# Expert products of a two-layer language-model tower on one core: the 64-row up products of a group issued together ahead of the 128-row ones, with six PSUM banks for up and one for down

## Chip, core and metric

The kernel runs on one core of a Trainium2 chip. The metric is device time in microseconds (us) of one execution. The kernel before takes 2085.38 us (median of 3 runs, 2085.08 to 2086.68).

## What is computed

The reference embeds 32 x 128 tokens in 192 dimensions and sends them through two layers, each an attention and a feed-forward part. Everything touched here lies in the last part, the mixture of experts of the second layer:

```python
T = B * S                                   # 4096 tokens, D = 192
logits = xm @ router_w.T + router_b         # E = 8 experts
topw, topi = jax.lax.top_k(softmax(logits), 2)
topw = topw / jnp.sum(topw, axis=-1, keepdims=True)
for e in range(E):
    h = gelu(xm @ w1[e] + b1[e], approximate=False)   # 192 -> 768
    y = h @ w2[e] + b2[e]                             # 768 -> 192
    out = out + combine[:, e:e + 1] * y
x = x + out
```

## The kernel before

**The expert part.** While layer 2 is computed, every token's normed row is written twice to a table in HBM (`xs`), ordered by expert. The expert part goes through this table in 39 groups (`NX`) of 256 rows (`NR`), each of one expert. Three groups make one turn of a hardware loop (`TURNS` is 13, `B3` is 3), and weights, rows, turned rows and outputs have three buffers each, number `h` for a group's place in its turn. All products are fp32; in the profile one fp32 `matmul` is two MATMUL records and two LDWEIGHTS records, and a transpose is one of each.

**A group's work.** The input dimension 192 is 128 + 64 and the hidden dimension 768 is six blocks of 128 (`FC`), taken in three pairs (`PAIRS`), blocks `p` and `p + 3`.

- SyncE (`sync_x`, L2245) loads the group's weights (L2258, six transfers) and its rows (L2262) three groups ahead: it waits for `x_out`, the end of the outputs of the group that had this buffer.
- VectorE `doubled` (L2217) copies the rows' last 64 columns when the rows have landed, so that both halves of the partitions get them.
- TensorE `turn_rows` (L2291, L2292) turns the next group's rows with four transposes into bank 6; ScalarE `take_rows` (L2350) takes them out as `x_T`, two instructions.
- TensorE `up` (L2296), once for each pair: two products of 128 rows (L2307, one for each block) and two of 64 rows (L2311). The two of 64 rows use partitions 0 to 63 and 64 to 127, so they lie in different halves of the array, and they end the sums that the two of 128 rows begin.
- ScalarE (L2359) applies gelu to the pair, two instructions, and counts `x_gelu`.
- TensorE `down` (L2315), once for each pair: four products of 128 rows and 192 columns (L2322), two row tiles `t` for each block, summed over the six blocks in banks 4 and 5.
- VectorE `outputs` (L2198) adds the weighted bias and the weighted result (L2204 to L2211), counts `x_out`, and GpSimd (`pool_x`, L2236) adds the rows into `moe_sum` in HBM with two indirect DMAs (L2240). It waits until both have landed before it takes the next group. An output buffer is used again three groups later, and `outputs` waits for that (L2200).

**What sets the order.** TensorE works in program order, written out in `group_of` (L2327): up 0, up 1, turn of the next group, down 0, up 2, down 1, down 2. Banks 0 and 1 serve pairs 0 and 2, banks 2 and 3 pair 1, so up 2 waits for the gelu of pair 0 (L2303). `down` waits for the gelu of its pair (L2316), and down 0 also for `x_out` of the group before (L2318), which frees banks 4 and 5. ScalarE takes the next group's rows between the gelus of pairs 1 and 2 (L2362).

```python
            def group_of(g, h, more, first=False):
                up(g, h, 0, first)
                up(g, h, 1)
                if more:
                    turn_rows(*((g, h + 1) if h < B3 - 1 else (g + 1, 0)))
                down(g, h, 0)
                up(g, h, 2)
                down(g, h, 1)
                down(g, h, 2)
```

Of the kernel before, what the change touches and what calls it, by code (L numbers as in the profile page):

```python
# [11 lines left out]
ACT = mybir.ActivationFunctionType  # L12
# [4 lines left out]
P = 128  # L17
T = 32
D = 192
# [6 lines left out]
TE, HE = 3, 64  # L26
# [9 lines left out]
def per(g, n, k):  # L36

    return g * n + k
# [57 lines left out]
def tower(nc, a, out):  # L96

    with ExitStack() as ctx:
# [2036 lines left out]
        B3 = 3  # L2135
# [33 lines left out]
        def vector_x(v, ch):  # L2169

            nc.vector.memset(amx[:, :], 0.0).then_inc(x_sel_r, 1)
            v.wait_ge(x_pos_p, 1)
            tot = bank[0][:, 400:400 + E]
            ch.step(nc.vector.tensor_scalar(x_steps, l_cnt[:, 0:NP], NR + 1 / 32, -NR - 3 / 64, ALU.mult, ALU.add))
            ch.step(nc.vector.tensor_tensor(x_more, tot.unsqueeze(2).to_broadcast([P, E, NP]),
                                            x_steps.unsqueeze(1).to_broadcast([P, E, NP]), ALU.is_gt))
            ch.step(nc.vector.tensor_reduce(x_ng, x_more, X, ALU.add))
            ch.step(nc.vector.tensor_copy(x_end, x_ng))
            for e in range(1, E):
                ch.step(nc.vector.tensor_tensor(x_end[:, e:e + 1], x_end[:, e:e + 1], x_end[:, e - 1:e], ALU.add))  # L2180
            group = l_cnt[:, 0:NX]
            ch.step(nc.vector.tensor_tensor(x_which, group.unsqueeze(2).to_broadcast([P, NX, E]),
                                            x_end.unsqueeze(1).to_broadcast([P, NX, E]), ALU.is_gt))
            ch.step(nc.vector.tensor_reduce(x_ex, x_which, X, ALU.add))
            nc.vector.tensor_scalar(x_from, x_ex, float(E - 1), None, ALU.min)
            ch.step(nc.vector.tensor_tensor(x_whose, x_which, x_ng.unsqueeze(1).to_broadcast([P, NX, E]), ALU.mult))
            nc.vector.tensor_copy(x_exi, x_from)
            ch.step(nc.vector.tensor_reduce(x_row, x_whose, X, ALU.add))
            ch.step(nc.vector.tensor_tensor(x_row, group, x_row, ALU.subtract))
            ch.step(nc.vector.tensor_scalar(x_row, x_row, -1.0, float(NR), ALU.add, ALU.mult))  # L2190
            ch.step(nc.vector.scalar_tensor_tensor(out=x_row, in0=x_ex, scalar=float(T * P), in1=x_row, op0=ALU.mult, op1=ALU.add))
            ch.step(nc.vector.tensor_scalar(x_row, x_row, float(E * T * P), None, ALU.min))
            nc.vector.tensor_copy(x_rowi, x_row).then_inc(x_read, 1)
            ch.step(nc.vector.memset(amx[:, :], 0.0))
            nc.vector.memset(amx[:, :], 0.0).then_inc(x_out, 1)
            ch.clear()

            def outputs(g, h, first=False):  # L2198
                if not first:
                    v.wait_ge(x_add, per(g, 32 * B3, 32 * (h - 2)))  # L2200
                w = lambda t: x_in[h][:, t, 1:2]
                v.wait_ge(x_w[h], per(g, 96, 96))
                for t in range(NT):
                    nc.vector.tensor_scalar(x_y[h][:, t, :], xb_2[h], w(t), None, ALU.mult)  # L2204
                ch.step(nc.vector.scalar_tensor_tensor(out=x_z[h], in0=x_in[h][:, :, 1], scalar=0.0, in1=r_dump, op0=ALU.is_equal,
                                                       op1=ALU.mult))
                ch.step(nc.vector.tensor_tensor(x_z[h], x_z[h], x_in[h][:, :, 0], ALU.max))
                nc.vector.tensor_copy(x_id[h], x_z[h])
                v.wait_ge(x_dn, per(g, B3, h + 1))
                for t in range(NT):  # L2210
                    ins = nc.vector.scalar_tensor_tensor(out=x_y[h][:, t, :], in0=bank[4 + t][:, 0:D], scalar=w(t),  # L2211
                                                         in1=x_y[h][:, t, :], op0=ALU.mult, op1=ALU.add)
                ins.then_inc(x_out, 1)

            def doubled(g, h):
                v.wait_ge(x_x[h], per(g, 16, 16))
                nc.vector.tensor_copy(x_in[h][:, :, WID:WID + HE], x_in[h][:, :, WID - HE:WID]).then_inc(x_dup, 1)  # L2217

            doubled(0, 0)
            for h in range(B3):  # L2220
                doubled(*((0, h + 1) if h < B3 - 1 else (1, 0)))
                outputs(0, h, True)
            ch.step(nc.vector.memset(amx[:, :], 0.0))
            ch.clear()
            with v.Fori(1, TURNS - 1) as g:
                for h in range(B3):
                    doubled(*((g, h + 1) if h < B3 - 1 else (g + 1, 0)))
                    outputs(g, h)
                ch.step(nc.vector.memset(amx[:, :], 0.0))
                ch.clear()  # L2230
            for h in range(B3):
                if h < B3 - 1:
                    doubled(TURNS - 1, h + 1)
                outputs(TURNS - 1, h)
# [10 lines left out]
        def sync_x(sp):  # L2245
# [35 lines left out]
            sp.dma_start(flat(out.rearrange("t p d -> (t p) d")), flat(acc[0:T * P, :])).then_inc(x_end_st, 16)  # L2281
            sp.wait_ge(x_end_st, 16)

        def tensor_x(pe):
            pe.wait_ge(x_sel_r, 1)
            nc.tensor.matmul(bank[0][:, 400:400 + E], r_ones, r_run, start=True, stop=True).then_inc(x_pos_p, 1)
# [6 lines left out]
                                             x_in[h][:, t, 2 + P:2 + 2 * P], ident[:, :])  # L2293
                mm.then_inc(x_turned, 1)

            def up(g, h, p, first=False):  # L2296
                if p == 0:
                    pe.wait_ge(x_xT, per(g, B3, h + 1))
                    pe.wait_ge(x_w[h], per(g, 96, 96))
                    if h > 0 or not first:  # L2300
                        pe.wait_ge(x_gelu, per(g, B3 * PAIRS, h * PAIRS))
                elif p == 2:
                    pe.wait_ge(x_gelu, per(g, B3 * PAIRS, h * PAIRS + 1))  # L2303
                b = (0, 2, 0)[p]
                for n in range(2):
                    q = p + PAIRS * n
                    nc.tensor.matmul(bank[b + n][:, 0:NR], xw_1a[h][:, q * P:(q + 1) * P], x_T[h][:, 0, :], start=True,  # L2307
                                     stop=False)
                for n in range(2):
                    s = slice(HE * n, HE * (n + 1))  # L2310
                    mm = nc.tensor.matmul(bank[b + n][:, 0:NR], xw_1b[h][s, p * P:(p + 1) * P], x_T[h][s, 1, :], start=False,  # L2311
                                          stop=True)
                mm.then_inc(x_up, 1)

            def down(g, h, p):  # L2315
                pe.wait_ge(x_gelu, per(g, B3 * PAIRS, h * PAIRS + p + 1))  # L2316
                if p == 0:
                    pe.wait_ge(x_out, per(g, B3, h + 1))  # L2318
                for n in range(2):
                    f = p + PAIRS * n  # L2320
                    for t in range(NT):
                        mm = nc.tensor.matmul(bank[4 + t][:, 0:D], x_hid[f][:, t * P:(t + 1) * P], xw_2[h][:, f, :],  # L2322
                                              start=(p == 0 and n == 0), stop=(p == PAIRS - 1 and n == 1))
                if p == PAIRS - 1:
                    mm.then_inc(x_dn, 1)

            def group_of(g, h, more, first=False):  # L2327
                up(g, h, 0, first)
                up(g, h, 1)
                if more:  # L2330
                    turn_rows(*((g, h + 1) if h < B3 - 1 else (g + 1, 0)))
                down(g, h, 0)
                up(g, h, 2)
                down(g, h, 1)
                down(g, h, 2)

            turn_rows(0, 0)
            for h in range(B3):
# [7 lines left out]
        def scalar_x(act):  # L2346
            def take_rows(g, h):
                act.wait_ge(x_turned, per(g, B3, h + 1))
                for c in range(2):
                    ins = nc.scalar.activation(x_T[h][:, c, :], bank[6][:, c * NR:(c + 1) * NR], ACT.Identity,  # L2350
                                               scale=x_ln2g[:, c:c + 1], bias=x_ln2b[:, c:c + 1])
                ins.then_inc(x_xT, 1)

            def group_of(g, h, more):
                for p in range(PAIRS):
                    act.wait_ge(x_up, per(g, B3 * PAIRS, h * PAIRS + p + 1))
                    for n in range(2):
                        q = p + PAIRS * n
                        ins = nc.scalar.activation(x_hid[q], bank[(0, 2, 0)[p] + n][:, 0:NR], ACT.Gelu,  # L2359
                                                   bias=xb_1[h][:, q:q + 1])  # L2360
                    ins.then_inc(x_gelu, 1)
                    if p == 1 and more:  # L2362
                        take_rows(*((g, h + 1) if h < B3 - 1 else (g + 1, 0)))

            take_rows(0, 0)
            with act.Fori(0, TURNS - 1) as g:
# [139 lines left out]
```

## Time and profile before

| what | value |
|---|---|
| median of 3 runs | 2085.38 us (2085.08 to 2086.68) |
| profiled execution: span from first to last instruction | 2106.3 us |
| profiled execution: own time | not given apart from its span |
| TensorE busy with matmuls, of the span | 1611.5 us (77%) |
| first and last start of an expert product of 64 rows (L2311) | 1722.3 us and 2084.3 us |
| 64-row, 128-row up and down MATMUL records | 468, 468 and 936 |

The profile shows one execution. It gives for each engine its instructions with start and duration, and for the idle time before one what ended it. A MATMUL record's end is modelled; successive matmuls overlap, so the pace of a stream is read from starts, or from the chain of waits, which gives each instruction only the time that it adds. PE stands for matmuls of TensorE, PEld for its weight loads, DVE for VectorE, ACT for ScalarE, POOL for GpSimd, SP for SyncE. All times are counted from the span's start. The profiled execution's span is 20.9 us longer than the median run.

### The profile page before, as it was taken

The numbers are of one execution on the slowest core, as the hardware profiler recorded it, in microseconds if no ns is written. First come the engines' busy times: TensorE is split into PE (matmuls) and PEld (weight loads), VectorE is DVE, ScalarE is ACT, GpSimd is POOL, SyncE is SP. The second block draws the span as 40 slices with busy tenths as digits, with TensorE's granted clock in tenths as the row PEclk, the third lists the DMA queues.
The fourth block names the chain that finished last, engine by engine and source line by source line (L and its number), as shares of the span: only waits on it lengthen the run. The fifth ranks groups of instructions, "written<-read, shape, count | busy, mean of one in ns | idle before, by whom it ended". The sixth has DMA issues, their size and how long they took to land.

```text
span 2106.3 us, 35471 instructions
## 1 busy us (share of the span) xinstructions
PE 1611.5 (77%) x12060; PEld 1159.8 (55%) x12060; DVE 1312.3 (62%) x4361; ACT 979.3 (46%) x2773; POOL 400.4 (19%) x494
## 2 busy tenths in 40 slices
PE   0166764968888578888888768888888759999996
PEld 0032223855665355555555456666676647777775
DVE  7898885878888677877788536555555532122221
ACT  1366998933444445554555323333333324443442
POOL 7302331000000100000000001222212223333332
PEclk9975555578888689999999878777777769999998
DMA  3000001079910000000000000000000037777775
GB/s 71 15 1 1 1 1 20 3 141 193 188 20 0 1 1 0 0 0 0 0 0 0 1 25 13 24 23 23 23 15 19 23 96 179 185 175 181 177 176 133
DMA packets 136262, 112.99 MB, mean 54 GB/s; under 512 B 29417, under 2 KB 128457, under 8 KB 136137
## 3 DMA queue, kind: packets, MB, share of 16 engines
q1 hardware_dynamic: 119320, 91.70, 18.4%
q0 software_dynamic: 16864, 20.33, 5.0%
q8 instruction: 40, 0.66, 0.1%
q14 instruction: 38, 0.30, 0.1%
HBM read 69.19 MB, written 45.94 MB: 55 GB/s over the span
## 4 chain that ended last, share of the span: by engine, by line
PE 52%; DVE 27%; ACT 14%; issue 4%; POOL 1%; DVEq 0%; DMA 0%; another core or an unknown queue 0%; SPq 0%; ACTq 0%; POOLq 0%
ACT bank L716 8%; PE bank L2322 8%; PE bank L1007 6%; PE bank L2307 5%; PE bank L2311 3%; PE bank L1987 3%; PE bank L966 3%; PE bank L1217 2%; PE bank L1665 2%; PE bank L1000 2%; PE bank L2000 2%; DVE WK L1839 1%; DVE WK L1581 1%; DVE R L1581 1%; DVE R L1839 1%
## 5 line engine op out<-in xcount | busy, mean ns | idle before, releaser
L1047 POOL TENSOR_TENSOR WK<-WK,mhalf 128x2 f32<-128x2 f32 (+1 forms) x96 | 77.9, 812 | 882.4 <-DVE WK L1505 328.4
L2359 ACT ACTIVATE R<-bank,R 128x256 f32<-128x256 f32 x234 | 98.2, 471 | 216.9 <-PE bank L2311 216.9
L2211 DVE SCALAR_TENSOR_TENSOR WK<-bank,R,WK 128x192 f32<-128x192 f32 x78 | 28.9, 413 | 262.8 <-PE bank L2322 262.8
L716 ACT ACTIVATE bank<-bank,nbias,sc 128x128 f32<-128x128 f32 x384 | 168.9, 991 | 22.6 <-POOL nbias L528 22.6
L1007 PE MATMUL bank<-WK,R 96*128 96x256 f32 x576 | 162.9, 429 | 17.0 <-ACT WK L973 11.0
L2240 POOL DMA_INDIRECT moe_sum<-WK x78 | 121.5, 1557 | 257.4 <-DVE WK L2211 196.4
L2322 PE MATMUL bank<-R 128*128 128x192 f32 x936 | 169.1, 331 | 0.0
L716 ACT ACTIVATION_READ_ACCUMULATOR bank<-bank,nbias,sc 128x1 f32 x384 | 163.0, 766 | 0.0
L2322 PEld LDWEIGHTS bank<-R 128*128 128x128 f32 x936 | 150.1, 190 | 13.3 <-issue 13.3
L1007 PEld LDWEIGHTS bank<-WK,R 96*128 96x128 f32 x576 | 116.2, 213 | 41.9 <-ACT WK L973 15.4
L2307 PE MATMUL bank<-R 128*128 128x256 f32 x468 | 125.2, 390 | 1.1 <-ACT R L2350 1.1
L1987 PE MATMUL bank<-WK 32*128 32x128 f32 x1536 | 84.4, 367 | 35.4 <-DVE R L1839 13.0
L610 PE MATMUL bank<-R 32*128 32x128 bf16 x384 | 62.7, 299 | 60.0 <-ACT bank L716 57.1
L966 PE MATMUL bank<-ident,WK 128*96 128x128 f32 x320 | 66.4, 345 | 44.3 <-DVE WK L1030 27.7
L1987 PEld LDWEIGHTS bank<-WK 32*128 32x128 f32 x1536 | 69.2, 255 | 50.5 <-DVE R L1839 15.3
L2307 PEld LDWEIGHTS bank<-R 128*128 128x128 f32 x468 | 84.0, 191 | 20.9 <-issue 13.3
L610 PEld LDWEIGHTS bank<-R 32*128 32x128 bf16 x384 | 29.4, 118 | 118.7 <-ACT bank L716 106.6
L1665 PE MATMUL bank<-WK,R 128*128 128x256 f32 x256 | 75.6, 420 | 15.0 <-ACT WK L993 15.0
L433 DVE TENSOR_REDUCE neg_all<-bank 128x3 f32<-128x384 f32 x128 | 69.4, 554 | 27.4 <-PE bank L610 25.2
L559 PE MATMUL bank<-R,wq 96*128 96x512 bf16 x192 | 79.3, 542 | 4.6 <-DVE WK L407 2.7
L2311 PE MATMUL bank<-R 64*128 64x256 f32 x468 | 82.7, 430 | 0.0
L1000 PE MATMUL bank<-R,WK 96*128 96x192 f32 x384 | 76.4, 343 | 2.9 <-ACT WK L973 1.4
(494 smaller groups left out, 3886.4 us busy)
## 6 DMA issues: line engine op xcount, KB each, us to landing
moe_rows_in<-zeros SPq DMA_DIRECT2D x1, 25026.0 KB, 138.7
R<-in_L_ffn_w SPq DMA_DIRECT2D x39, 576.0 KB
R<-in_L_ffn_w SPq DMA_DIRECT2D x39, 384.0 KB
R<-moe_rows_in SPq DMA_DIRECT2D x39, 194.0 KB, 4.6
R<-in_L_ffn_w SPq DMA_DIRECT2D x78, 96.0 KB
R<-in_L_ffn_b SPq DMA_DIRECT2D x39, 96.0 KB
moe_sum<-resid POOLq DMA_DIRECT2D x16, 192.0 KB
moe_sum<-WK POOLq DMA_INDIRECT x78, 5.9
```

The lines of the kernel that those rows point to most:

```text
L610: mm = nc.tensor.matmul(bank[u % 4][:, k * P:(k + 1) * P], qk[32 * j:32 * j + 32, k, i * P:(i + 1) * P], qk[32 * j:32 * j + 32, 3 + k, i * ...
L716: ins = nc.scalar.activation(s, s, ACT.Exp, bias=nbias[:, u, k:k + 1], scale=col(SS), accum_out=units(sum_all, g, u)[:, k:k + 1])
L966: mm = nc.tensor.transpose(a.bank[b][0:C, c * NM + i * P:c * NM + (i + 1) * P], src[:, i, c * C:(c + 1) * C], ident[:, :])
L1000: mm = nc.tensor.matmul(a.bank[b][:, i * D:(i + 1) * D], a.xT[0:C, c, i * P:(i + 1) * P], w[0:C, c, :], start=(c == 0), stop=(c == 1))
L1007: mm = nc.tensor.matmul(out, w[0:C, c, m], a.xT[0:C, c, :], start=(c == 0), stop=(c == 1))
L1665: nc.tensor.matmul(a.bank[c][:, out], wa[:, c * P:(c + 1) * P], a.xT[:, 0, :], start=True, stop=False)
L1987: mm = nc.tensor.matmul(a.bank[j][:, k * P:(k + 1) * P], x, y, start=True, stop=True)
L2240: pool.indirect_dma_start(out=acc, out_offset=bass.IndirectOffsetOnAxis(ap=x_id[k % B3][:, t:t + 1].bitcast(U32), axis=0), in_=x_y[k % B3] ...
L2307: nc.tensor.matmul(bank[b + n][:, 0:NR], xw_1a[h][:, q * P:(q + 1) * P], x_T[h][:, 0, :], start=True, stop=False)
L2311: mm = nc.tensor.matmul(bank[b + n][:, 0:NR], xw_1b[h][s, p * P:(p + 1) * P], x_T[h][s, 1, :], start=False, stop=True)
L2322: mm = nc.tensor.matmul(bank[4 + t][:, 0:D], x_hid[f][:, t * P:(t + 1) * P], xw_2[h][:, f, :], start=(p == 0 and n == 0), stop=(p == PAIRS ...
L2359: ins = nc.scalar.activation(x_hid[q], bank[(0, 2, 0)[p] + n][:, 0:NR], ACT.Gelu, bias=xb_1[h][:, q:q + 1])
```

## The change

TensorE's order within a group becomes: all six 64-row products first (they now begin the sums), in three pairs, then the six 128-row ones, pair by pair (they end the sums and count `x_up`), then the turn of the next group's rows, then down 0, 1 and 2. The three pairs of up products have banks 0 to 5. The down products of both row tiles go to bank 7, columns 0 to 191 and 192 to 383; only the first of them has `start`. ScalarE does the gelus of all three pairs and then takes the next group's rows. The wait of up 2 for a gelu is gone; the 64-row products wait for the turned rows, the weights and all gelus of the group before, as up 0 did.

```diff
-                    ins = nc.vector.scalar_tensor_tensor(out=x_y[h][:, t, :], in0=bank[4 + t][:, 0:D], scalar=w(t),
+                    ins = nc.vector.scalar_tensor_tensor(out=x_y[h][:, t, :], in0=bank[7][:, t * D:(t + 1) * D], scalar=w(t),
...
+        def hidden_at(p, n):
+
+            return bank[2 * p + n][:, 0:NR]
...
-            def up(g, h, p, first=False):
-                if p == 0:
-                    pe.wait_ge(x_xT, per(g, B3, h + 1))
-                    pe.wait_ge(x_w[h], per(g, 96, 96))
-                    if h > 0 or not first:
-                        pe.wait_ge(x_gelu, per(g, B3 * PAIRS, h * PAIRS))
-                elif p == 2:
-                    pe.wait_ge(x_gelu, per(g, B3 * PAIRS, h * PAIRS + 1))
-                b = (0, 2, 0)[p]
+            def up_rests(g, h, first=False):
+                pe.wait_ge(x_xT, per(g, B3, h + 1))
+                pe.wait_ge(x_w[h], per(g, 96, 96))
+                if h > 0 or not first:
+                    pe.wait_ge(x_gelu, per(g, B3 * PAIRS, h * PAIRS))
+                for p in range(PAIRS):
+                    for n in range(2):
+                        s = slice(HE * n, HE * (n + 1))
+                        nc.tensor.matmul(hidden_at(p, n), xw_1b[h][s, p * P:(p + 1) * P], x_T[h][s, 1, :], start=True, stop=False)
+
+            def up(h, p):
                 for n in range(2):
                     q = p + PAIRS * n
-                    nc.tensor.matmul(bank[b + n][:, 0:NR], xw_1a[h][:, q * P:(q + 1) * P], x_T[h][:, 0, :], start=True,
-                                     stop=False)
-                for n in range(2):
-                    s = slice(HE * n, HE * (n + 1))
-                    mm = nc.tensor.matmul(bank[b + n][:, 0:NR], xw_1b[h][s, p * P:(p + 1) * P], x_T[h][s, 1, :], start=False,
-                                          stop=True)
+                    mm = nc.tensor.matmul(hidden_at(p, n), xw_1a[h][:, q * P:(q + 1) * P], x_T[h][:, 0, :], start=False, stop=True)
                 mm.then_inc(x_up, 1)
...
-                        mm = nc.tensor.matmul(bank[4 + t][:, 0:D], x_hid[f][:, t * P:(t + 1) * P], xw_2[h][:, f, :],
-                                              start=(p == 0 and n == 0), stop=(p == PAIRS - 1 and n == 1))
+                        mm = nc.tensor.matmul(bank[7][:, t * D:(t + 1) * D], x_hid[f][:, t * P:(t + 1) * P], xw_2[h][:, f, :],
+                                              start=(p == 0 and n == 0 and t == 0), stop=(p == PAIRS - 1 and n == 1),
+                                              skip_group_check=True)
...
             def group_of(g, h, more, first=False):
-                up(g, h, 0, first)
-                up(g, h, 1)
+                up_rests(g, h, first)
+                for p in range(PAIRS):
+                    up(h, p)
                 if more:
                     turn_rows(*((g, h + 1) if h < B3 - 1 else (g + 1, 0)))
-                down(g, h, 0)
-                up(g, h, 2)
-                down(g, h, 1)
-                down(g, h, 2)
+                for p in range(PAIRS):
+                    down(g, h, p)
...
-                        ins = nc.scalar.activation(x_hid[q], bank[(0, 2, 0)[p] + n][:, 0:NR], ACT.Gelu,
-                                                   bias=xb_1[h][:, q:q + 1])
+                        ins = nc.scalar.activation(x_hid[q], hidden_at(p, n), ACT.Gelu, bias=xb_1[h][:, q:q + 1])
                     ins.then_inc(x_gelu, 1)
-                    if p == 1 and more:
-                        take_rows(*((g, h + 1) if h < B3 - 1 else (g + 1, 0)))
+                if more:
+                    take_rows(*((g, h + 1) if h < B3 - 1 else (g + 1, 0)))
```

## Rows read from the trace of the kernel before

**Rows 1.** The page: span, busy time, slices, the chain by engine.

```profile
span 2106.3 us, 35471 instructions
...
PE   0166764968888578888888768888888759999996
...
PEclk9975555578888689999999878777777769999998
...
PE 52%; DVE 27%; ACT 14%; issue 4%; POOL 1%; DVEq 0%; DMA 0%; another core or an unknown queue 0%; SPq 0%; ACTq 0%; POOLq 0%
```

**Rows 2.** Busy time by stretch: PE, PEld, DVE, ACT, POOL, clock, DMA share, GB/s.

```profile
1880.00:1920.00 40.00, 40.00 (x224) 31.04 (x223) 8.66 (x36) 16.27 (x34) 12.42 (x8) 1.00 0.73 180
...
1881.30:1890.67 9.37, 9.37 (x54) 7.23 (x54) 1.91 (x8) 4.71 (x9) 3.10 (x2) 1.00 0.72 175
...
2040.00:2086.00 46.00, 46.00 (x255) 35.28 (x255) 9.28 (x40) 16.22 (x38) 15.61 (x10) 1.00 0.57 126
```

**Rows 3.** Chain of waits through one group: start, time it adds, instructions.

```profile
1881.62 0.86 PE bank L2307 x4
1882.48 0.63 PE bank L2311 x4
1883.11 1.06 PE bank L2307 x4
...
1884.81 0.26 PE bank L2291
1885.07 0.11 PE bank L2292
...
1885.39 1.30 PE bank L2322 x8
1886.70 0.86 PE bank L2307 x4
...
1888.19 2.80 PE bank L2322 x16
```

**Rows 4.** Durations of 64-row matmuls; a run of 32-row ones; their line's groups.

```profile
L2311 PE MATMUL bank<-R x468: 376/480/792, 1722.3 to 2084.3; 64*128 64x256 f32 x156
...
1559.49 1.67 PE L1987 MATMUL bank<-WK 32*128 32x128 f32 x24
...
L1987 PE MATMUL bank<-WK 32*128 32x128 f32 x480 | 26.9, 372 | 10.6 <-DVE R L1839 5.7 <-DVE WK L1839 3.1 <-DVE R L1870 1.1
...
L1987 PEld LDWEIGHTS bank<-WK 32*128 32x128 f32 x480 | 22.0, 260 | 15.2 <-DVE R L1839 6.5 <-DVE WK L1839 3.7 <-issue 3.0
```

**Rows 5.** Timeline of ScalarE in the same group.

```profile
1884.85 0.84 ACT L2359 ACTIVATE R<-bank,R 128x256 f32<-128x256 f32 x2 [0.85 <-PE bank L2311]
1885.58 1.02 ACT L2350 ACTIVATE R<-bank,R 128x256 f32<-128x256 f32 x2
...
1889.10 1.28 ACT L2359 ACT_TABLE_LOAD   x1
```

**Rows 6.** VectorE in the same group, and its waits for rows from 1750 to 2080.

```profile
1881.65 0.74 DVE L2211 SCALAR_TENSOR_TENSOR WK<-bank,R,WK 128x192 f32<-128x192 f32 x2 [6.63 <-PE bank L2322]
1882.95 0.23 DVE L2217 COPY R<-R 128x128 f32<-128x128 f32 x1 [0.55 <-DMA R<-moe_rows_in]
...
DVE R L2217 <- DMA R<-moe_rows_in: 21.2, 32, 1.2
```

**Rows 7.** GpSimd's adds: timeline, landing times (min/median/max), waits, and issues at the end.

```profile
1883.16 1.55 POOL L2240 DMA_INDIRECT moe_sum<-WK  x1 [5.96 <-DVE WK L2211]
1885.01 1.55 POOL L2240 DMA_INDIRECT moe_sum<-WK  x1 [0.30 <-issue]
...
DMA to landing us min/median/max: 3.3/5.9/7.2
...
POOL moe_sum L2240 <- DMA moe_sum<-WK: 35.7, 6, 6.0
...
moe_sum<-WK POOLq DMA_INDIRECT x6, 3.5
```

## The prediction

> **What bounds the kernel now.** The page comes first [rows 1]: the six slices that lie wholly in the expert part, the 34th to the 39th of 40, show TensorE busy for nine tenths or more and its granted clock at nine tenths or more, while the half-clock stretches lie earlier. The table by stretch says it sharply [rows 2]: in every stretch of the expert part TensorE's matmuls fill the whole time (40.00 of 40.00, 46.00 of 46.00 us) at clock 1.00, the 2.4 GHz level, while VectorE, ScalarE and GpSimd are at a fifth, two fifths and a third, and the DMA engines at 0.73. So this part lasts as long as TensorE's own list of matmuls takes, and only what shortens that list counts. The chain of waits then prices the list piece by piece [rows 3]; the group from 1881.62 takes 9.37 us.
>
> Its pieces, in order: up 0 is 0.86 for the 128-row records and 0.63 for the 64-row ones; up 1 is 1.06 and 0.63; the turn 0.26 and three times 0.11; down 0 1.30; up 2 0.86 and 0.63; downs 1 and 2 2.80. Sum 9.36. Equal work is not priced equally: four 128-row records are 0.86 (0.215 each) where they follow other 128-row work (up 0 and up 2, both after a down), but 1.06 after 64-row work. Sixteen down records after 64-row work are 2.80, though eight are 1.30 after a transpose, so 2.60 was due. The first transpose is 0.26 against 0.11. And a 64-row block is 0.63 where its halves, running side by side, stream two records' time, 0.43. **Each passage between 64-row and 128-row work thus costs about 0.20 us** (0.15 before a transpose); the group has six. It isn't a wait for a bank: the transposes write bank 6 and the downs bank 4, which the 64-row products before them do not touch, and both pay; up 2 after down 0 changes banks and pays nothing. Part of it is seen in the records: the first matmuls of a 64-row block last 480 ns and the later ones 376 [rows 4], so about 0.10 is a weight load that nothing hides, and the rest the emptying of the array.
>
> **The change part by part.**
>
> *The order on TensorE.* The same records are issued, in two runs instead of six. New group: 64-row pairs 0.63 + 0.43 + 0.43 = 1.49; 128-row pairs 1.06 + 0.86 + 0.86 = 2.78; turn 4 x 0.11 = 0.44; downs 3 x 1.30 = 3.90. Sum 8.61 against 9.36, so **0.75 us a group**. With 39 groups (468 MATMUL records of 64 rows, twelve a group [rows 4]) that is 29.3 us. Worked out the other way, by taking 0.20 for each of the four passages that go, it is 31.2; I take the first, as it prices the transposes' passage at its own row. The price that no row shows directly is the 64-row pair that follows another pair: 0.43 if its loads hide behind the pair before. Bounds: 0.43 (nothing but streams) and 0.53 (each new pair shows the 0.10 of load). The nearest row is a run of 32-row products, 24 records in 1.67 us [rows 4]: four quarters of the array side by side, in six rounds. Less one record's length of 0.37 that is 0.22 a round, under the 0.26 of a single load there, so loads into a busy quarter are hidden. I take 0.43.
>
> *What down 0 waits for.* The gelus of pair p cover 0.84 us [rows 5], and up delivers pairs 0.86 apart, so ScalarE keeps pace. Counted as the chain counts, from the group's start: up 0 is out at 2.6, its gelu done at 3.5, and down 0 has its place from 4.7 (its first load some 0.3 earlier); gelu 1 is done at 4.3, needed at 5.7; gelu 2 at 5.2, needed at 7.0. At least 0.9 us cover each. The two output instructions of the group before end 0.8 us after the group's start [rows 6], also long before down 0. The removed wait of up 2 had cost nothing.
>
> *take_rows after the third gelu.* It starts at 5.2 and takes 1.02 [rows 5], done at 6.2, and the next 64-row products want it at 8.3: cover 2.1. The table load of 1.28 us [rows 5], once a turn, then ends at 7.5, and the next gelu starts at 11.2. Cost nothing; without the cover it would be what take_rows is late.
>
> *The turn, and the rows it needs.* It moves from 3.2 to 4.3 us after the group's start. Rows are asked for by the outputs three groups back, and a group is 0.75 shorter, so the copy on VectorE comes later within its group: now it waits at most 1.2 us after the outputs [rows 6] and ends 2.2 us after the group's start at the latest, then near 3.0. The slack before the turn stays at about 1 us at worst. Behind the turn only the downs are queued. VectorE has time: 1.9 us of work in 9.37 [rows 2].
>
> *SyncE and the DMA engines.* The same loads in less time: 0.72 of 9.37 is 6.7 us of work, or 0.78 of 8.61. No new instruction, nothing is moved past another there.
>
> *Bank 7 for both row tiles.* VectorE reads the same number of elements. TensorE already sends records in direct succession into one bank (the two passes of each product), so I cost it at nothing, with 0 to 0.02 a record as bounds: a full 0.02 x 24 x 39 = 19 us would be seen at once.
>
> *GpSimd, the one cover that gets thin.* A group's adds are two issues 1.86 us apart, the second landing 5.9 (median) to 7.2 us (longest) after it [rows 7]: 7.8 to 9.1 from the first issue, and some 0.3 to the next (what lies between the two issues). In the window of the waits row the landing ended GpSimd's wait only 6 times; else the outputs did, at a pace of 9.37. At 8.61 it will be the landing more often. The range is 8.1 to 9.4, and I take 8.7, since the second issue, behind the first, should land later than the median of both. GpSimd may fall behind without hurting anyone (output buffers return three groups later), and after the last loads the landings take 3.5 [rows 7], so that some 2.5 us a group is caught up in three groups, 7.5 in all. The lag at 8.7 is 35 x 0.09 = 3: nothing is left at the end.
>
> *Sum.* 29.3 us. The profiled span is 2106.3 and the execution's own time is not given apart from it, so the sum is made as a difference: 2106.3 becomes 2077.0. The span stands 1.0% above the median run; the same difference from 2085.4 gives **2056 us** (29.0 if it shrinks with that ratio).
>
> **A rule against this.** In the 64-row pair the second set of loads does not delay its matmuls: the block costs 0.43 plus one passage [rows 3], and six rounds of 32-row work run through [rows 4]. The Trainium skill, in "TensorE: Matmul & The Clock Gate", Part 3, says that a weight load overlaps running matmuls only when it targets another row group. By that rule the pairs put next to each other would each show their loads; the rows speak against it, and it is kept as rival B.
>
> **Rivals.**
>
> *A, GpSimd sets the pace.* Denser DMA traffic lengthens the landings, and the adds take 9.0 to 9.4 us a group. For it: six waits already end on a landing. Against it: traffic of a group is one burst, and a lagging GpSimd lands in its gap. The last add then comes 35 x (9.2 - 8.61) - 7.5 = 13 us late: 2069 (2062 at 9.0, 2076 at 9.4). Chance 0.13.
>
> *B, loads of 64-row pairs show.* Two more unhidden loads of 0.10 a group, 8 us: 2064. Chance 0.05.
>
> *C, the change does not do what it says.* If the 0.20 hung on something else than the passage (the sums of one bank, say), it would return in the new order: 2085. The transposes and downs that pay without sharing a bank speak against it. Chance 0.02.
>
> *D, slower.* The same GpSimd wait, past its point of decision: all adds a group over 8.61 + (29.3 + 7.5) / 35 = 9.66 us. With landings at 7.2 x 0.78 / 0.72 = 7.8 each time, a group takes 1.86 + 7.8 + 0.3 = 9.96, which gives 35 x 1.35 - 7.5 = 40 us on 2056: 2096. It needs the longest landing in every group. Chance 0.03.
>
> **How the numbers follow.** The main case has 0.77, and its own spread is 2053 (31.2 saved and a little at the first group, where up 2 now runs ahead of rows that are late) to 2060 (a part of bank 7's bound). The range takes in B and the middle of A: 2052 to 2069. Within 0.2% (4 us, about what a measurement can tell from no change) lies C: 0.02. Slower is D: 0.03. Faster 0.95.
>
> **What would show it.** In the chain of waits after: one 64-row piece of twelve records at about 1.5 us a group, then twelve 128-row up records at about 2.8, a first transpose at 0.11, and 3.9 for 24 down records; 8.6 us a group with TensorE still filling each stretch. ScalarE's take_rows after three gelus with more than 2 us before the next group. GpSimd's waits ended by landings more often, by outputs less. B would show as 1.7 in the 64-row piece; A as a chain that ends in DMA and GpSimd over many groups, and more than 7 us between TensorE's last matmul and the copy of the result. TensorE idle before the turn for late rows, or a group above 8.8 us, would make the prediction wrong.

## The result, and the profile after

The changed kernel takes 2055.7 us (median of 4 runs, 2055.25 to 2057.09), the kernel before 2086.0 (4 runs, 2085.08 to 2086.8): a ratio of 0.9855, interval 0.9841 to 0.9869. That is 30 us less, where 29.3 were forecast.

Busy time by stretch, after (columns: stretch, PE, PEld, DVE, ACT, POOL, clock, DMA share, GB/s):

```profile
1830.00:1838.62 8.62, 8.62 (x53) 7.61 (x53) 2.11 (x8) 3.44 (x8) 2.73 (x2) 1.00 0.81 194
...
1780.00:1820.00 40.00, 40.00 (x245) 35.59 (x246) 8.56 (x35) 17.44 (x39) 13.73 (x9) 1.00 0.81 199
```

Against [rows 2] nothing has changed its place: TensorE still fills every microsecond at clock 1.00. Only the list is shorter, 8.62 us a group instead of 9.37. The DMA engines were busy for 0.68 to 0.75 of each stretch of 40 us inside the expert part, and are so now for 0.78 to 0.81 (0.78 forecast). The chain of waits, after, through one group:

```profile
1824.18 3.90 PE bank L2323 x24
1828.08 1.50 PE bank L2308 x12
1829.58 2.79 PE bank L2313 x12
1832.36 0.11 PE bank L2295
1832.47 0.11 PE bank L2296
1832.58 0.11 PE bank L2295
1832.69 0.11 PE bank L2296
```

The reader sees each term of the sum: 1.50 for the twelve 64-row records (1.49 forecast), 2.79 for the 128-row up records (2.78), four times 0.11 for the turn, whose first transpose cost 0.26 in [rows 3], and 3.90 for the downs. The three 0.63 pieces of [rows 3] have become one piece that pays the 0.20 of a passage once.

How far the covers hold, from the timeline of the same group (start, length, instructions, idle time before and what ended it):

```profile
1828.12 0.74 DVE L2211 SCALAR_TENSOR_TENSOR WK<-bank,R,WK 128x192 f32<-128x192 f32 x2 [5.05 <-PE bank L2323]
...
1829.62 1.55 POOL L2240 DMA_INDIRECT moe_sum<-WK  x1 [5.21 <-DMA moe_sum<-WK]
1829.98 0.23 DVE L2217 COPY R<-R 128x128 f32<-128x128 f32 x1 [1.10 <-DMA R<-moe_rows_in]
...
1830.67 2.57 ACT L2360 ACTIVATE R<-bank,R 128x256 f32<-128x256 f32 x6 [3.84 <-PE bank L2313]
...
1832.20 0.27 PE L2295 MATMUL bank<-ident,R 128*128 128x128 f32 x1
...
1832.64 4.07 PE L2323 MATMUL bank<-R 128*128 128x192 f32 x24
1833.13 1.02 ACT L2351 ACTIVATE R<-bank,R 128x256 f32<-128x256 f32 x2
1836.63 1.57 PE L2308 MATMUL bank<-R 64*128 64x256 f32 x12
```

The six gelu instructions run as one piece of 2.57 us and end at 1833.24; the next group's rows are taken by 1834.15, and TensorE wants them at 1836.63: 2.5 us of cover, 2.1 forecast. The copy of the rows ends at 1830.21, 2.0 us before the turn; from the third group on this slack is 1.0 to 3.2 us, 1.9 in the median. The waits, after, from 1730 to 2025 (who waited for what: us in total, times, longest):

```profile
POOL moe_sum L2240 <- DMA moe_sum<-WK: 161.3, 31, 6.0
DVE R L2217 <- DMA R<-moe_rows_in: 41.1, 34, 2.1
POOL moe_sum L2240 <- DVE WK L2211: 15.6, 3, 5.2
```

Against the 6 waits of [rows 7], 31 of GpSimd's are now ended by a landing, as forecast, and yet no time was lost to it. Most of them cost GpSimd nothing either: in 25 of the 39 groups the adds begin at most 0.8 us after the outputs end, which is also the usual time in the kernel before, where the outputs decide; in the other 14 they begin up to 0.9 us later than that. VectorE waits for rows up to 2.1 us, 0.9 longer than in [rows 6].

**Two profiles that differ elsewhere.** The two spans differ by 52.6 us (2106.3 and 2053.7), far more than the 30 us of the runs. The first copy of the expert part stands at 1717.8 us before and at 1694.7 after, though no instruction ahead of it was changed (rows of the copies and of the outputs, before and then after, durations and first and last start):

```profile
L2217 DVE COPY R<-R x39: 217/227/242, 1717.8 to 2070.4; 128x128 f32<-128x128 f32 x39
...
L2211 DVE SCALAR_TENSOR_TENSOR WK<-bank,R,WK x78: 406/413/419, 1731.7 to 2087.8; 128x192 f32<-128x192 f32 x78
```

```profile
L2217 DVE COPY R<-R x39: 226/227/428, 1694.7 to 2020.0; 128x128 f32<-128x128 f32 x39
...
L2211 DVE SCALAR_TENSOR_TENSOR WK<-bank,R,WK x78: 406/412/419, 1707.4 to 2035.0; 128x192 f32<-128x192 f32 x78
```

From first copy to last output it is 370.0 us before and 340.3 after: 29.7 us is what the expert part gained. The other 23 arose ahead of it, 22 of them in layer 2, whose 64 reductions of L1839 into WK run from 1237.1 to 1643.4 us before and from 1237.8 to 1622.0 after. The changed kernel profiled once more (below) has its first copy at 1686.0, so this part varies by some microseconds between executions of the same code.

### The profile page after: what moved, and what is told of

It is laid out like the page before. It is cut to its first block, busy times and chain, and to the rows that moved or that the text cites. A ratio compares the mean times of both kernels' runs of the same rounds, so it can differ in the third digit from the quotient of the medians.

```text
span 2053.7 us, 35471 instructions
## 1 busy us (share of the span) xinstructions
PE 1576.5 (77%) x12060; PEld 1171.7 (57%) x12060; DVE 1312.4 (64%) x4361; ACT 980.1 (48%) x2773; POOL 399.9 (19%) x494
## 4 chain that ended last, share of the span: by engine, by line
PE 52%; DVE 28%; ACT 14%; issue 4%; POOL 1%; DVEq 0%; DMA 0%; ACTq 0%; POOLq 0%; SPq 0%
ACT bank L716 8%; PE bank L2323 7%; PE bank L1007 6%; PE bank L2313 5%; PE bank L2308 3%; PE bank L1987 3%; PE bank L966 3%; PE bank L1217 2%; PE bank L1665 2%; PE bank L1000 2%; PE bank L2000 2%; DVE WK L1839 2%; DVE WK L1581 1%; DVE R L1581 1%; DVE R L1839 1%
## 5 line engine op out<-in xcount | busy, mean ns | idle before, releaser
L2211 DVE SCALAR_TENSOR_TENSOR WK<-bank,R,WK 128x192 f32<-128x192 f32 x78 | 28.9, 412 | 208.9 <-PE bank L2323 208.9
L2323 PE MATMUL bank<-R 128*128 128x192 f32 x936 | 158.6, 326 | 0.0
L2313 PE MATMUL bank<-R 128*128 128x256 f32 x468 | 111.5, 388 | 0.0
L1987 PE MATMUL bank<-WK 32*128 32x128 f32 x1536 | 83.5, 364 | 20.3 <-DVE WK L1839 6.0
L2089 ACT ACTIVATE WK<-bank,R 128x256 f32<-128x256 f32 x96 | 40.3, 470 | 77.7 <-PE bank L1007 77.7
```

What stands on the lines that cost most here:

```text
L1987: mm = nc.tensor.matmul(a.bank[j][:, k * P:(k + 1) * P], x, y, start=True, stop=True)
L2313: mm = nc.tensor.matmul(hidden_at(p, n), xw_1a[h][:, q * P:(q + 1) * P], x_T[h][:, 0, :], start=False, stop=True)
L2323: mm = nc.tensor.matmul(bank[7][:, t * D:(t + 1) * D], x_hid[f][:, t * P:(t + 1) * P], xw_2[h][:, f, :], start=(p == 0 and n == 0 and t == ...
```

## The experiments

Every run carries a trace, and the stretch from the first to the last output instruction (L2211) is free of what varies ahead of it. For the 38 groups between, the changed kernel takes 327.6 us and the kernel before 356.1. The ratios are to runs of the kernel before on the same chip.

| kernel | ratio (interval) | median us | outputs, first to last | against changed |
|---|---|---|---|---|
| before | 1 | 2086.0 | 356.1 | +28.5 |
| changed | 0.9855 (0.9841 to 0.9869) | 2055.7 | 327.6 | 0 |
| six passages | 0.9990 (0.9975 to 1.0005) | 2084.0 | 357.8 | +30.2 |
| four passages | 0.9932 (0.9915 to 0.9948) | 2071.4 | 342.7 | +15.1 |
| 128-row products first | 0.9855 (0.9838 to 0.9871) | 2054.0 | 326.0 | -1.6 |
| one bank alone | 1.0001 (0.9992 to 1.0011) | 2086.1 | 356.1 | +28.5 |
| same half | 1.0104 (1.0087 to 1.0120) | 2104.3 | 376.5 | +48.9 |
| turn early | 0.9957 (0.9941 to 0.9974) | 2073.9 | 348.7 | +21.1 |
| GpSimd plus 1 | 0.9854 (0.9838 to 0.9871) | 2052.1 | 327.5 | -0.1 |
| GpSimd plus 2 | 0.9855 (0.9839 to 0.9871) | 2052.0 | 327.6 | 0 |
| GpSimd plus 3 | 0.9847 (0.9828 to 0.9866) | 2053.1 | 327.5 | -0.1 |
| GpSimd plus 4 | 0.9864 (0.9842 to 0.9886) | 2053.7 | 327.6 | 0 |
| 128-row first, again | 0.9845 (0.9827 to 0.9862) | 2051.0 | 326.0 | -1.6 |
| changed, again | 0.9835 (0.9818 to 0.9853) | 2048.1 | 327.5 | -0.1 |

### Are the passages the whole gain?

Six passages a group, all else as changed:

```diff
-                up_rests(g, h, first)
                 for p in range(PAIRS):
+                    up_rests(g, h, (p,), first)    # the 64-row products of pair p alone
                     up(h, p)
```

> The changed kernel with its six banks and its bank 7, its turn and its downs in place, but the 64-row products of each pair issued directly before the 128-row ones of the same pair: six passages between 64-row and 128-row work a group in place of two, everything else as changed. Theory P (a passage costs 0.20 us and nothing else of the change matters): 4 x 0.20 x 39 = 31.2 us on the changed kernel's 2055.7, so 2087, just above the kernel before. Rival L (the gain came from the removed gelu wait, the free banks or the later turn, which all stay): about 2056. Rival T (ScalarE or GpSimd bound part of it): between.

Four passages:

```diff
-                up_rests(g, h, first)
-                for p in range(PAIRS):
-                    up(h, p)
+                for pairs in ((0, 1), (2,)):
+                    up_rests(g, h, pairs, first)
+                    for p in pairs:
+                        up(h, p)
```

> As the last, but in two runs: 64-row products of pairs 0 and 1, their 128-row ones, then both of pair 2. Four passages a group. Theory P: 2 x 0.20 x 39 = 15.6 us on 2055.7, so 2071.3: the cost is linear in passages. Rival (a passage costs only where a sum's two parts follow each other in one bank): one such place a group, at most 7.8 us, so 2064 or less.

Measured: 30.2 us more for four passages added and 15.1 for two, over 38 groups 0.20 us a passage both times. Rivals L and T are out: with the new banks, the later turn and the missing gelu wait all kept, the gain is gone. So is the rival of the shared bank, which allowed 7.8 us for four passages. The chain of waits with six passages:

```profile
1857.05 0.63 PE bank L2309 x4
1857.68 1.06 PE bank L2314 x4
1858.74 0.63 PE bank L2309 x4
1859.37 1.06 PE bank L2314 x4
```

Each piece is back at the price that [rows 3] has after a passage. The chain of waits with four passages:

```profile
1853.36 1.06 PE bank L2309 x8
1854.42 1.92 PE bank L2314 x8
1856.35 0.63 PE bank L2309 x4
1856.98 1.06 PE bank L2314 x4
```

At 0.215 us for each record's stream, two of the 64-row ones side by side, every piece is its streams and 0.20, whatever its length. About 0.10 of it shows in the records: the first 64-row records of a piece last 0.48 us and the later ones 0.38 [rows 4]. That this half is a weight load that nothing hides, and the rest the emptying of the array, remains a reading: no run takes the two apart. The Trainium skill, in "TensorEngine Tiling (Array Packing)", Key Properties, states that a change of tiling mode drains TensorE. The trace fits that, with 0.20 us for this change each way.

### Must the 64-row products come first?

```diff
                 for p in range(PAIRS):
-                    up(h, p)                       # ends the sums, counts x_up
+                    up(g, h, p, first)             # begins the sums
+                up_rests(h)                        # ends them, counts x_up for each pair
```

> Two passages as in the changed kernel, but the six 128-row up products come first (they begin the sums), then the 64-row pairs, which end them and count the pairs 0.43 us apart. The passage back is now in front of the transposes, priced at 0.15 rather than 0.20. Theory P: 0.05 x 39 = 2 us less, 2053.7, if the gelus keep up: out at 3.2, 3.7 and 4.1 us, gelus done at 4.1, 4.9 and 5.8, needed at 4.4, 5.7 and 7.0, so the first has only 0.3 us of cover. Rival G (that cover is not there and down 0 waits for the first gelu): 0.1 to 0.5 us a group, 2058 to 2075. Either way the saving does not need the 64-row products to come first, only to be together.

The trace bears out the term and shows no gelu wait. Chain of waits, 128-row products first:

```profile
1856.82 2.59 PE bank L2316 x12
1859.41 1.50 PE bank L2304 x12
1860.90 0.26 PE bank L2295
```

Up has lost its 0.20 (2.59 against 2.79) and the transpose pays 0.15: 1.6 us less over 38 groups. The ratios can't resolve it, so this kernel and the changed one were timed side by side:

> The kernel with the 128-row products first once more, on one chip with the changed kernel. Its trace gave 8.577 us a group against 8.622, so theory P says 1.7 us less than the changed kernel (0.1%), which the medians of five rounds may or may not show; a difference of more than 4 us either way would mean something that the traces do not show.

> The changed kernel itself, beside the last: 30 us under the kernel before, 1.7 us over the last.

The traces repeat themselves (326.0 and 327.5 us), but the ratios came the other way round, 0.9845 and 0.9835, with intervals that overlap for the greater part. The order within up is a matter of 0.1% and below what these runs can tell. No kernel here beats the changed one beyond doubt.

### Does the shared output bank cost anything?

The kernel before with the down products and the outputs' reading moved to bank 7, and nothing else.

```diff
-    matmul(bank[4 + t][:, 0:D], ..., start=(p == 0 and n == 0), ...)
+    matmul(bank[7][:, t * D:(t + 1) * D], ..., start=(p == 0 and n == 0 and t == 0), ...)
```

> The kernel before with only the down products of both row tiles put into bank 7, in its old order. Theory P: no cost and no gain, 2086, the same as before within 0.1%. Rival (records in succession into one bank are delayed by 0.02 us each, the upper bound of the prediction): up to 19 us more, 2105; then the changed kernel would have hidden a loss in its sum.

No: ratio 1.0001, and 356.1 us between the outputs, as before. The down pieces keep their price in the chain of waits:

```profile
1855.59 1.30 PE bank L2322 x8
...
1858.39 2.80 PE bank L2322 x16
```

The bound of 19 us in the prediction falls away.

### Do loads of the 64-row products hide behind each other?

Both 64-row products of a pair on the same half of the array. The second block's product uses the weights and rows of partitions 0 to 63, so this kernel computes something else.

```diff
-                        s = slice(HE * n, HE * (n + 1))
+                        s = slice(0, HE)
```

> The changed kernel with both 64-row products of a pair taken from partitions 0 to 63 (weights and rows), so the second block's product has the wrong half of the weights and the output is not the reference's. Both now use the same half of the array, so they cannot run side by side: six more records' streams of 0.215 us a group. Theory S (loads into a busy half hide behind the stream before): 6 x 0.215 x 39 = 50 us on 2055.7, so 2106, with the 64-row piece at 2.8 us. Rival B (a load waits until its half is free, 0.10 us each as at a passage): ten more such loads, another 1.0 us a group, 2145, with the piece at 3.8 us.

Measured: 48.9 us over 38 groups, 1.29 a group, which is 6 x 0.215. The chain of waits with both on one half:

```profile
1854.63 3.90 PE bank L2323 x24
1858.53 2.78 PE bank L2308 x12
```

Twelve records in 2.78 us, which is 12 x 0.215 and one passage of 0.20: no load behind the first shows. Rival B is out: by it, this piece would have been 3.8 us, ten loads of 0.10 more, and the changed kernel's own piece 1.7 instead of 1.50. The Trainium skill, in "TensorE: Matmul & The Clock Gate", Part 3, says in its list of what overlaps that a load overlaps running matmuls only in another row group. That does not hold here, and the measurement decides. "The mechanism", in the same part of the Trainium skill, also names a load into the background weight buffer as one that is pulled ahead; the measurement would fit that, but no run here shows where a load goes. The run also prices the two halves side by side: they save 1.29 us a group, more than putting the products together.

### Is the later place of the turn needed?

```diff
                 up_rests(g, h, first)
+                if more:
+                    turn_rows(*((g, h + 1) if h < B3 - 1 else (g + 1, 0)))
                 for p in range(PAIRS):
                     up(h, p)
-                if more:
-                    turn_rows(*((g, h + 1) if h < B3 - 1 else (g + 1, 0)))
```

> The changed kernel with the turn of the next group's rows directly behind the 64-row products, 2.8 us earlier in the group. By the trace after, the copy of the rows ends 10.1 us after the outputs three groups back, and the turn comes 12.0 us after them: 1.9 us of slack, which 2.8 us overdraws. Both hang on the same loop, so the group settles at the length at which the turn meets the rows: 8.62 - 1.9 + 2.8 = 9.5 us. Theory: 0.9 x 35 = 31 us on 2055.7, about 2087, with TensorE idle before the turn, ended by VectorE's copy, some 0.9 us a group. Rival (rows come sooner when the DMA engines have more time, or the wait is hidden by the slower group): less than 10 us.

It costs 21.1 us, two thirds of what was expected. The timeline of TensorE with the turn early:

```profile
1854.42 1.57 PE L2308 MATMUL bank<-R 64*128 64x256 f32 x12
1857.18 0.33 PE L2295 MATMUL bank<-ident,R 128*128 128x128 f32 x1 [1.19 <-DVE R L2217]
...
1865.92 0.33 PE L2295 MATMUL bank<-ident,R 128*128 128x128 f32 x1
```

The mechanism is as said: TensorE waits before the turn for VectorE's copy of late rows. Its idle time before the turns, from the third on, adds up to 20.9 us, which is about the whole loss. It does not come in each group alike: the next turn, at 1865.92, waits for nothing. The size was off, and one cause can be worked out: I counted the idle time once. From the outputs three groups back to the turn, TensorE passes two turns, the one of the group between and the one that waits. An idle time s before each turn gives the rows 2s more, so the missing 0.9 us is made up by a group that is 0.45 us longer. Measured are 21.1 / 38 = 0.56 us. The remaining 0.11 is not explained; the count takes one slack of 1.9 us for all groups, where it varied from 1.0 to 3.2. The changed order needs its turn behind the up products.

### When does GpSimd decide?

One to four small powers behind each group's wait for its landings:

```diff
                 pool.wait_ge(x_add, 32 * (k + 1))
+                for m in range(4):                 # 1, 2, 3, 4
+                    nc.gpsimd.tensor_tensor(spare[:, ...], mhalf[:, 0:1], mhalf[:, 0:1], ALU.pow)
```

> The changed kernel with one small power on GpSimd (0.69 to 0.72 us in the trace before) behind each group's wait for its landings. The adds of a group now take some 8.16 + 0.3 + 0.75 = 9.2 us against TensorE's 8.62. Theory A (GpSimd may lag, and only the lag left at the end counts, less 7.5 us caught up behind the last loads): 35 x 0.6 - 7.5 = 13 us, about 2069. Rival (its start-up of 0.76 us already overlaps the wait for the landings, and landings get shorter when they fall in the gap of the loads): at most 3 us, 2056 to 2059.

> As the last with two such powers, 9.9 us of work on GpSimd a group. Theory A: the lag grows by 1.3 us a group, reaches the 14 us at which the output buffers run out after about 11 groups, and from there GpSimd sets the pace of all engines: 35 x 1.3 - 7.5 = 38 us, about 2094, slower than the kernel before, with VectorE waiting for the landings of three groups back. Rival as for the last: under 15 us.

> The changed kernel with three powers of 0.57 us on GpSimd behind each wait for the landings. With two of them the second landing took 5.4 us from its issue and the lag stayed near 2 us, so GpSimd fell into step with the loads. Theory S (it stays in step only as long as its work fits 8.62 us): issues 1.86, second landing 5.4 or a little less, 0.07, powers 1.7, restart 0.17: 9.1 to 9.2, too long by 0.5, so the lag grows by 0.5 us a group to some 15 us and is caught up only in part behind the last load: about 10 us longer than the changed kernel, TensorE's group still 8.62, all of it in the time after TensorE's last matmul. Rival E (landings shorten further, as they did for two): no change again.

> As the last with four powers, 9.7 us on GpSimd a group. Theory S: the lag grows by 1.1 us a group, reaches the 14 us at which the outputs wait for their buffer after some 13 groups, and then all engines go at GpSimd's 9.7: about 33 us longer than the changed kernel, which is slower than the kernel before, with VectorE's L2204 waiting for the landings. That would be the prediction's slower rival, produced on purpose. Rival E: under 10 us.

All four went against theories A and S: the outputs keep 327.5 or 327.6 us, and with four powers the delay of the adds behind the outputs does not grow but settles at 3.3 us in the median (0.76 in the changed kernel). Something is left at the end: with four powers the adds of the last group begin 2.7 us after its outputs, and from the last output instruction to the end of the span it is 20.3 us, against 18.7 and 18.3 in the two traces of the changed kernel. That is about 2 us that the column of outputs can't show, far from the 33 of theory S. The medians of four powers and of the changed kernel again, on one chip, are 5.6 us apart, with ranges that overlap (2049.6 to 2058.3 and 2046.2 to 2052.7).

Landing times of both issues of a group together, from issue (min/median/max), changed and with four powers:

```profile
DMA to landing us min/median/max: 3.5/5.8/7.2
```

```profile
DMA to landing us min/median/max: 3.4/4.8/5.8
```

And the chain of waits with four powers (it runs through GpSimd at its end):

```profile
1852.49 4.10 DMA moe_sum<-WK
1856.59 0.07 issue
1856.66 2.19 POOL spare L2247 x4
1858.85 0.19 issue
1859.04 1.58 POOL moe_sum L2242
1860.62 0.30 issue
1860.92 4.56 DMA moe_sum<-WK
```

The four powers are 2.19 us of new serial work, and the period is still 1860.92 - 1852.49 = 8.43 us here. What gave way is the landing of the second issue, the one that GpSimd waits for last. Taken apart by issue, in medians over the 39 groups (us; "after the outputs" counts from the end of the group's output instructions; the last column leaves out the three groups behind the last loads, whose landings take 3.5):

| kernel | second issue, after the outputs | its landing, from the issue | its landing, after the outputs |
|---|---|---|---|
| before | 2.6 | 6.4 | 9.2 |
| changed | 2.6 | 6.3 | 9.1 |
| plus 1 | 3.2 | 5.9 | 9.1 |
| plus 2 | 3.8 | 5.3 | 9.2 |
| plus 3 | 4.6 | 4.8 | 9.5 |
| plus 4 | 5.2 | 4.3 | 9.6 |

The second issue goes out 2.6 us later with four powers, and lands 0.5 us later. The first issue's landing hardly changes (5.4 and 5.0). So GpSimd's loop closes in both kernels: 1.86 + 6.3 and at least 0.27 to the next issue are 8.4 us, which fit into 8.62 without powers; with four, 1.89 + 4.3 + 2.4 (the powers and the 0.26 around them) are 8.6. The start-up of an issue takes no more of the loop than that, though 0.76 us lie between the end of the outputs and the adds where the outputs decide (1829.62 against 1828.86).

## Why the prediction was right

**The sum.** Each of its terms is in the trace after at its forecast value: 8.62 us a group against 8.61. The experiments confirm what the terms rested on: 0.20 us for a passage, linear in their number, without a share for banks, the gelu wait or the turn. The one term with no row of its own, 0.43 for a 64-row pair behind another, was taken rightly, but partly by luck. The prediction divided 24 records in 1.67 us, less one record's 0.37, by six rounds and got 0.22. Six rounds have five intervals, which makes it 0.26, no less than the 0.26 of a load, and by these numbers nothing was shown to hide. The records themselves do show it: there the second round starts 0.38 us after the first and each later one 0.21 after the last, and the later records last 0.42 each, not 0.37. The doubled stream on one half settles it: even loads into the same half hide.

**The covers.** Gelus and rows in time as worked out. The slack before the turn stayed at 2.0 us in the group shown and at 1.0 at its least, as forecast, and moving the turn shows what it is worth. Bank 7 cost nothing.

**The rivals.** B is refuted by the 1.50 us piece and the same-half run, C by the runs with six and four passages, and A and D by the four runs with longer work on GpSimd. One step of the prediction was wrong although it did not move the total: GpSimd was costed as a chain of fixed pieces (1.86 + landing + 0.3), giving a pace of 8.7, a lag of 3 us at the end and a decision point of 9.66. In the changed kernel the pieces add up to 8.4, under TensorE's 8.62, and there was no growing lag. A's premise, that denser traffic lengthens the landings, did not come true: the second landing takes 6.3 us, and 6.4 before. And by fixed pieces the 2.19 us of four powers on 8.4 would have made 10.6 a group, well past 9.66, and a kernel slower than the one before, where the group stayed at 8.62. The landing time was read as a property of the transfer, but it changes with the moment of its issue. The chance of 0.16 for A and D together, and most of the range above 2060, stood on that.

**The spans.** The sum was made as a difference, and rightly: the profiled execution before was long in a part that the change does not touch.

## What to carry to other kernels

Count the passages between matmuls of different row tiling in a TensorE-bound loop, and price one by comparing equal instructions in the chain of waits; where banks allow, gather the small-row products into one run. Such a reordering moves other work, so check what each moved step needs: here a turn 2.8 us earlier gave back three quarters of the gain. And don't add up the pieces of a loop over DMAs as fixed when one of them is a landing time under traffic: take the landing that the loop waits for by itself, count it from a fixed point of the group as well as from its issue, and lengthen the loop in a run to see whether anything moves.

## What was not expected

- A landing under traffic keeps its place in the group rather than its length. Whether the second issue goes out 2.6 or 5.2 us after the outputs, it lands 9.1 to 9.6 us after them, and 2.19 us of added serial work on GpSimd left the kernel's pace unchanged. That the adds wait behind the group's loads, and get through as these run out, fits these numbers and the 3.5 us of a landing without loads [rows 7]. The group's last load itself lands 9.8 us after the outputs in the changed kernel and 8.9 with four powers. The cause was not tested by itself, for instance by holding the loads back.
- A power of one element a partition took 0.54 to 0.58 us here (medians of the four runs), not the 0.7 assumed from the kernel before.
- Layer 2 took 22 us more in the profiled execution before than in the one after, over L1839's 64 reductions, with the same code and the same mean clock of 0.74 from 1238 to 1686 us. What makes it vary is open.
